# Eight stores of image rows issued in the next stage, and one square root moved between two copies

## The chip, the cores and the metric

The kernel runs on one core of a Trainium2 chip. The metric is the device time of one launch in microseconds (us), the median of several runs. A core has five engines, each with its own instruction stream: TensorE (PE in the rows; its weight loads are PEld), VectorE (DVE), ScalarE (ACT), GpSimd (POOL) and SyncE (SP), which in this kernel issues most of the DMAs. The engines wait for each other through semaphores only.

## The reference, cut to what matters

The model embeds 32 images and 32 texts and passes the joined rows through a mixer layer and a layer of 8 experts. The change lies in the embedding:

```python
x = x.reshape(B, C, h, P, w, P)                       # 32 images, 14 x 14 patches of 3 x 16 x 16
x = jnp.transpose(x, (0, 2, 4, 3, 5, 1)).reshape(B, h * w, P * P * C)
x = _layernorm(x, ln1_g, ln1_b)
x = jnp.einsum('bnp,pd->bnd', x, W_proj) + b_proj     # 768 -> 192
x = _layernorm(x, ln2_g, ln2_b)
x = jnp.concatenate([cls, x], axis=1) + pos_embedding
...
h = jnp.concatenate([image_rows, text_rows(x_txt, itok)], axis=1)
h = h + mixer(_layernorm(h))
h = h + experts(_layernorm(h))
```

## The kernel before, in words

The stages follow one another: embed_images, embed_text, normalise_in, mix, project_route, experts. Each is a function that opens one Block with an instruction list for each engine. At a Block's end all engines meet (a barrier, recorded on line 92 or 551 where the timeline names it), so a stage begins when the last engine has arrived.

embed_images takes the images in NGRP = 4 groups of GB = 8. Partition r of a tile holds patch row r // 8 of image r % 8, so a tile has 112 partitions. The 14 patch columns of a group are done one after the other, w = 0 to 13, in two alternating buffers. For each column

- ScalarE normalises the patches (normalise, L276);
- TensorE transposes them into PSUM (turn, L328, 6 transposes);
- ScalarE copies them out in two halves (take, L283 and L284); it waits for the transposes and for the projection two columns earlier;
- TensorE projects them (project, L336, 6 matmuls, recorded as 12 instructions); it waits for take of this column (turned_out) and for VectorE to have emptied the PSUM buffer of the column two before (y_taken);
- VectorE adds the bias into yg (y_take, L426) and gathers statistics (y_stat, L431).

The second normalisation needs the variance of the projected columns: VectorE computes it (y_moments, L403 to L410), ScalarE takes the square root (root_y, L289), VectorE the reciprocal (y_scales, L415) and then scales all columns (scale_mul L437, scale_add L444) and makes the statistics that the next stage wants (scale_stats, L451, which counts row_done). For the last group this is done in two parts, columns 0 to 9 (CUT = 10) and 10 to 13. VectorE's order at the end is: y_moments(0, CUT), take of columns 10 and 11, y_scales, then take of column 12 and the scaling of columns 0 to 9, take of column 13, and the second part.

SyncE writes yg to the intermediate h0 in DRAM: for each group eight DMAs, one an image (L220), for the last group eight for columns 0 to 9 when row_done says so, and eight for columns 10 to 13. yg and its completion semaphores y_out live on through embed_text. ScalarE at the end writes the class row (L318) and waits for that DMA.

In embed_text SyncE issues 12 small loads of weights (L631 to L643; among them win_row and wout_row, which TensorE transposes on L858 and L863), then waits for text rows to store (L649), and at its end waits for y_out. VectorE and TensorE build prefix sums, then text rows go in eight steps of four texts through ScalarE's Gelu (L818).

The order before at ScalarE's end of the image stage, and SyncE's:

```python
                if g + 1 == NGRP:
                    root_y(g, 0, CUT)
                for j in range(2):
                    take(g * GRID + GRID - 2 + j, j)
```

Of the kernel before, what the change touches and what calls it, by code (L numbers as in the profile page):

```python
# [29 lines left out]
GRID = IMG // PATCH  # L30
NIMG = GRID * GRID
# [3 lines left out]
LP = NCHUNK * Q  # L35
# [26 lines left out]
HR = D + 6  # L62
# [5 lines left out]
GB = 8  # L68
GP_ROWS = GB * GRID
NY = 3  # L70
NGRP = B // GB
PD = PATCH * PATCH * CH
BORDER = (0, 4, 1, 5, 2, 6, 3, 7)
# [4 lines left out]
def bank(nc, ctx, name, shape):  # L78

    t = ctx.enter_context(nc.psum_tensor(name, [128, 512], F32))  # L80
    n = 1
    for s in shape[1:]:
        n *= s
    v = t[0:shape[0], 0:n]
    if len(shape) == 3:
        v = v.rearrange("p (a b) -> p a b", a=shape[1])
    return v


def embed_images(nc, io, dr, keep):  # L90

    with ExitStack() as ctx:
# [3 lines left out]
        def sem(name):  # L96
            return ctx.enter_context(nc.semaphore(name))

        R = GP_ROWS
# [12 lines left out]
        yg = keep["yg"]  # L112
# [20 lines left out]
        vint = sb("vint", [128, 2, NVAR // 128], I32)  # L133

        ps_t = [[bank(nc, ctx, f"ps_t{j}{k}", [128, 3, R]) for k in range(2)]
                for j in range(2)]
        ps_y = [bank(nc, ctx, f"ps_y{j}", [R, D]) for j in range(2)]
        ps_b = bank(nc, ctx, "ps_b", [R, D])
        ps_i = bank(nc, ctx, "ps_i", [TXT, 2, B])

# [16 lines left out]
        row_done = sem("row_done")  # L157
        tick = keep["tick"]
        y_out = keep["y_out"]
# [19 lines left out]
        h0 = dr["h0"]  # L179
# [3 lines left out]
        @block.sync  # L183
        def _(sp):
            def whole(g):
                for b in BORDER:
                    sp.dma_start(xg[g][b:R:GB, :, :].rearrange("r (c p) w -> r c (p w)", c=CH),
                                 xv[g * GB + b].rearrange("h c p w -> h c (p w)")).then_inc(x_in[g % 2][0], 16)

            whole(0)  # L190
            sp.dma_start(vt[:, :, 0:NF], io["L0_txt_var_family_onehot"].rearrange("(p j) f -> p j f", p=128)
                          ).then_inc(tab, 16)
            for n, name in enumerate(["var_outer_norm", "var_inner_norm", "var_has_outer", "var_has_inner"]):
                sp.dma_start(vcol[:, n, :], io["L0_txt_" + name].rearrange("(p j) -> p j", p=128)).then_inc(tab, 16)
            for n, name in enumerate(["var_family_id", "var_group_id"]):
                sp.dma_start(vint[:, n, :], io["L0_txt_" + name].rearrange("(p j) -> p j", p=128)).then_inc(tab, 16)
            for b in BORDER:
                sp.dma_start(pos[b:R:GB, :, :].rearrange("r w d -> r (w d)"),
                             posv[0, 1:1 + NIMG, :].rearrange("(h w) d -> h (w d)", w=GRID)).then_inc(pos_in, 16)
            sp.dma_start(cls[:, 0, :], posv[0, 0, :].partition_broadcast(B)).then_inc(pos_in, 16)  # L200
            sp.dma_start(cls[:, 1, :], io["L0_tok_cls_token"][0, 0, :].partition_broadcast(B)).then_inc(pos_in, 16)
            whole(1)
            sp.wait_ge(tab, TAB_MADE)
            sp.dma_start(dr["var_tab"].rearrange("(p j) f -> p (j f)", p=128), vt[:].rearrange("p j f -> p (j f)")
                          ).then_inc(tab, 16)
            tables.store(sp)
            for g in range(2, NGRP):
                for n, (lo, hi) in enumerate(PIECES):
                    sp.wait_ge(x_normed, GRID * (g - 2) + hi)
                    for b in BORDER:  # L210
                        for c in range(CH):
                            sp.dma_start(xg[g % 2][b:R:GB, c * PATCH:(c + 1) * PATCH,
                                                   lo * PATCH:hi * PATCH],
                                         xv[g * GB + b][:, c, :, lo * PATCH:hi * PATCH]).then_inc(x_in[g % 2][n], 16)
            for g in range(NGRP):
                for lo, hi in ((0, GRID),) if g + 1 < NGRP else ((0, CUT), (CUT, GRID)):
                    sp.wait_ge(row_done, GRID * g + hi)
                    for b in BORDER:
                        row = (g * GB + b) * LP + 1
                        sp.dma_start(h0[row:row + NIMG, :].rearrange("(h w) d -> h (w d)", w=GRID)[:, lo * HR:hi * HR],  # L220
                                     yg[g % NY][b:R:GB, lo:hi, :].rearrange("r w d -> r (w d)")
                                     ).then_inc(y_out[min(g, 1)], 16)

        @block.gpsimd
        def _(pool):
# [29 lines left out]
        @block.scalar  # L255
        def _(act):
            for n, name in enumerate(("x_txt", "itok_BS_0_4095")):
                act.dma_start(idr[:, n, :], io[name]).then_inc(ids, 16)
            act.dma_start(wp[:, :, :, :].rearrange("p n c d -> p n (c d)"), wv).then_inc(w_in, 16)
            with nc.allow_non_contiguous_dma(reason="per-feature vectors of a few values"):  # L260
                act.dma_start(g1[:], gv).then_inc(w_in, 16)
                act.dma_start(b1[:], bv).then_inc(w_in, 16)
            for tile, name in ((bias1, "L0_tok_b_proj"), (g2, "L0_tok_ln2_g"), (b2, "L0_tok_ln2_b")):
                act.dma_start(tile[:], io[name].partition_broadcast(R)).then_inc(w_in, 16)
            act.wait_ge(misc, 1)
            act.dma_start(h0.rearrange("(b t) d -> b t d", t=LP)[:, L:LP, :].rearrange("b t d -> b (t d)"),
                          zrow[:]).then_inc(misc, 16)

            tables.functions(act)

            def root(g):
                act.wait_ge(x_std, g + 1)
                act.activation(rs[g % 2][:], ve[g % 2][:], ACT.Sqrt).then_inc(x_sqrt, 1)

            def normalise(g, w, j):
                act.activation(xc[j][:], xg[g % 2][:, :, bass.ds(w * PATCH, PATCH)], ACT.Identity,  # L276
                               bias=nb[g % 2][:, bass.ds(w, 1)], scale=rs[g % 2][:, bass.ds(w, 1)]
                               ).then_inc(x_normed, 1)

            def take(i, j):  # L280
                act.wait_ge(turned, i + 1)
                act.wait_ge(projected, i + 1)
                act.copy(xt[j][:, 0:3, :], ps_t[j][0][:])  # L283
                act.copy(xt[j][:, 3:6, :], ps_t[j][1][:]).then_inc(turned_out, 1)  # L284

            act.sem_inc(projected, 2)
            def root_y(n, lo=0, hi=GRID):
                act.wait_ge(y_var, n + 1)
                act.activation(rsy[:, lo:hi], vey[:, lo:hi], ACT.Sqrt).then_inc(y_sqrt, 1)  # L289

            def steps(g, lo, hi):
                with act.Fori(lo, hi) as p:
                    for j in range(2):
                        take(g * GRID + 2 * p + j, j)
                        normalise(g, 2 * p + 2 + j, j)

            root(0)
            act.wait_ge(x_rstd, 1)
            normalise(0, 0, 0)
            normalise(0, 1, 1)  # L300
            for g in range(NGRP):
                steps(g, 0, EARLY)
                if g:
                    root_y(g - 1)
                steps(g, EARLY, GRID // 2 - 1)
                if g + 1 == NGRP:
                    root_y(g, 0, CUT)
                for j in range(2):
                    take(g * GRID + GRID - 2 + j, j)
                    if g + 1 < NGRP:  # L310
                        if j == 0:
                            root(g + 1)
                            act.wait_ge(x_rstd, g + 2)
                        normalise(g + 1, j, j)
            root_y(NGRP, CUT, GRID)
            act.wait_ge(misc, 1 + 16)
            act.wait_ge(cls_ok, 1)
            act.dma_start(h0.rearrange("(b t) d -> b t d", t=LP)[:, 0, :], cls_row[:]).then_inc(misc, 16)  # L318
            act.wait_ge(misc, 1 + 32)
# [222 lines left out]
CUT = 2 * LATE  # L542
# [3 lines left out]
def embed_text(nc, io, dr, keep):  # L546
# [4 lines left out]
    with ExitStack() as ctx:  # L551
# [78 lines left out]
        def _(sp):  # L630
# [10 lines left out]
            sp.dma_start(wi[HD:HD + 1, 1, :], io["L0_attn_b_in"].unsqueeze(0)).then_inc(p_in, 16)  # L641
            for n in range(2):
                sp.dma_start(wout_row[:, n, :], io["L0_attn_W_out"][n * HD:(n + 1) * HD, :]).then_inc(p_in, 16)  # L643
            hv = dr["h0"].rearrange("(b t) d -> t b d", t=LP)
            for n in range(NG4):
                sp.wait_ge(rows_done, n + 1)
# [1698 lines left out]
```

## Time and profile before

| | us |
|---|---|
| median of 3 runs | 1410.48 (1410.46 to 1414.09) |
| the profiled execution's own time | 1408.07 |
| its span | 1406.3 |
| TensorE busy | 1166.0 (83%) |
| VectorE busy | 807.6 (57%) |
| ScalarE busy | 690.2 (49%) |
| GpSimd busy | 389.6 (28%) |

The profile comes from one execution. Times in it count from the span's start. A row of a timeline gives the start in us, the time in us from the beginning of the first to the end of the last of the instructions merged in it, engine, line, operation, the tile written and the tiles read, the number of instructions (x), and in brackets the engine's idle time before it with what ended it. SPq and ACTq are DMA issues on the queues of SyncE and ScalarE. The granted clock of TensorE is given as a share of full speed: 1.00 is 2.4 GHz, 0.50 is 1.2 GHz. Releasers are inferred from semaphore events.

### The profile page before, as it was taken

How to read it: one execution, taken by the hardware profiler on the slowest of the kernel's cores; microseconds unless marked ns; L12 is line 12 of the kernel's file. 1: busy time of each engine (PE TensorE's matmuls, PEld its weight loads, DVE VectorE, ACT ScalarE, POOL GpSimd, SP SyncE). 2: the span in 40 equal slices, each digit the busy share in tenths (PEclk: the TensorE clock that was granted, in tenths of full speed). 3: DMA queues.
4: the chain of work that ended last, by engine and by line, in shares of the span. 5: the costliest groups of instructions: out<-in, count | busy, mean ns of one | idle time of the engine just before them, and what ended most of it. 6: DMA issues, size and time to landing. Idle time of an engine off the chain costs nothing. (4 is left out here: it accounts for less than half of the span.)

```text
span 1406.3 us, 38278 instructions
## 1 busy us (share of the span) xinstructions
PE 1166.0 (83%) x11847; PEld 1098.3 (78%) x11847; DVE 807.6 (57%) x2553; ACT 690.2 (49%) x1544; POOL 389.6 (28%) x358
## 2 busy tenths in 40 slices
PE   0398993466579999999999499993799999999996
PEld 0398992244469898898898399983799999999996
DVE  0778976773842633534536368775455555666653
ACT  2265660255652332232233256652567777777774
POOL 6877000001100300201103015555123333333332
PEclk9999996576699998998999899995899999999998
DMA  8766312003410423333233689982111111111110
GB/s 189 178 102 147 98 36 68 23 0 121 209 27 14 92 79 76 69 99 77 64 98 80 185 255 305 296 256 79 33 43 42 45 42 42 45 45 45 45 45 13
DMA packets 166427, 133.83 MB, mean 95 GB/s; under 512 B 77989, under 2 KB 155932, under 8 KB 164704
## 3 DMA queue, kind: packets, MB, share of 16 engines
q1 hardware_dynamic: 152352, 112.22, 29.8%
q0 software_dynamic: 10384, 17.49, 3.9%
q10 hardware_dynamic: 3600, 3.01, 0.7%
q8 instruction: 45, 0.74, 0.2%
q14 instruction: 46, 0.38, 0.1%
HBM read 89.97 MB, written 43.53 MB: 95 GB/s over the span
## 5 line engine op out<-in xcount | busy, mean ns | idle before, releaser
L2125 POOL DMA_INDIRECT out_dram<-ob,oi x89 | 127.2, 1429 | 291.8 <-DVE ob L2179 288.8
L2235 PE MATMUL ph<-zt,wc 64*128 64x128 f32 x3204 | 197.4, 274 | 3.1 <-ACT zt L2137 1.4
L2235 PEld LDWEIGHTS ph<-zt,wc 64*128 64x128 f32 x3204 | 191.6, 189 | 6.9 <-issue 3.6
L2227 PE MATMUL py<-w2c,ht 64*128 64x192 f32 x2136 | 194.1, 327 | 1.5 <-DVE yb L2177 1.5
L1492 PE MATMUL pa<-wi,xn 96*85 (+3 forms) x2048 | 185.6, 246 | 3.0 <-POOL mc L1344 2.8
L1492 PEld LDWEIGHTS pa<-wi,xn 96*85 96x85 f32 (+1 forms) x2048 | 180.2, 155 | 4.4 <-POOL mc L1344 3.1
L2150 ACT ACTIVATE ht<-ph,bc 128x128 f32<-128x128 f32 x534 | 156.9, 371 | 48.5 <-PE ph L2235 48.5
L2227 PEld LDWEIGHTS py<-w2c,ht 64*128 64x128 f32 x2136 | 172.6, 187 | 2.0 <-issue 1.9
L1355 POOL TENSOR_TENSOR bd<-rr,mc 128x656 f32<-128x656 f32 x48 | 61.5, 1282 | 306.9 <-PE pb L1510 187.1
L1366 DVE COPY x<-pa 85x384 f32<-85x384 f32 x100 | 55.3, 553 | 146.0 <-PE pa L1492 146.0
L336 PE MATMUL ps_y<-wg,xt 128*112 128x192 f32 x672 | 124.2, 337 | 13.6 <-DVE yg L426 9.5
L2144 ACT COPY w2c<-w2e 128x1152 f32 x89 | 102.6, 1152 | 59.4 <-PE py L2227 59.0
L336 PEld LDWEIGHTS ps_y<-wg,xt 128*112 128x112 f32 x672 | 111.0, 183 | 15.2 <-DVE yg L426 10.5
L1538 PEld LDWEIGHTS pa<-gp,x 85*128 85x128 f32 x768 | 101.0, 207 | 15.0 <-issue 9.2
L1742 POOL DMA_INDIRECT xs<-row,sli x82 | 82.3, 1004 | 96.7 <-DVE row L1996 36.4
L1538 PE MATMUL pa<-gp,x 85*128 85x128 f32 x768 | 102.3, 292 | 7.4 <-issue 6.2
L1822 PE MATMUL p<-wo,y 128*128 128x192 f32 x492 | 93.0, 341 | 0.5 <-DVEq L1916 0.5
L1385 ACT ACTIVATE yt<-pa 96x384 f32<-96x384 f32 (+1 forms) x84 | 44.6, 531 | 98.8 <-PE pa L1552 91.3
L328 PE MATMUL ps_t<-ident,xc 112*128 112x112 f32 x336 | 43.2, 266 | 54.5 <-ACT xc L276 54.5
L1822 PEld LDWEIGHTS p<-wo,y 128*128 128x128 f32 x492 | 82.6, 197 | 0.7 <-DVEq L1916 0.7
L328 PEld LDWEIGHTS ps_t<-ident,xc 112*128 112x128 f32 x336 | 39.0, 146 | 56.1 <-ACT xc L276 54.7
L2164 DVE TENSOR_SCALAR z<-xr 128x192 f32<-128x192 f32 x89 | 33.8, 379 | 74.6 <-DMA xr<-xs 74.6
(318 smaller groups left out, 1966.2 us busy)
## 6 DMA issues: line engine op xcount, KB each, us to landing
y<-yd SPq DMA_DIRECT2D x41, 384.0 KB, 4.7
gp<-kd SPq DMA_DIRECT2D x48, 246.0 KB, 2.8
xg<-in_x SPq DMA_DIRECT2D x16, 588.0 KB
xr<-xs SPq DMA_DIRECT2D x89, 98.0 KB, 1.9
yd<-yt SPq DMA_DIRECT2D x56, 144.0 KB, 1.9
hb<-h SPq DMA_DIRECT2D x41, 192.0 KB, 5.6
yd<-yt SPq DMA_DIRECT2D x40, 192.0 KB, 2.1
xg<-in_x SPq DMA_DIRECT2D x48, 112.0 KB
```

What stands on the lines that cost most here:

```text
L328: t = pe.transpose(ps_t[j][k // 3][:, k % 3, :], flat[:, k * 128:(k + 1) * 128], keep["ident"][0:R, 0:R])
L336: m = pe.matmul(ps_y[j][:], xt[j][:, k, :], wg[:, k, :], start=(k == 0), stop=(k == KC - 1))
L1355: pool.tensor_tensor(bd[g % 2][:], rr[g % 2][:, :].unsqueeze(1).to_broadcast([128, GE, Q]), mc[:, bass.ds(n, 1), :].rearrange("p a e -> p ...
L1492: mm = pe.matmul(p[:, i * EB:(i + 1) * EB], xn[0:rows, f, b, c * Q:c * Q + W], keep["wi"][0:rows, f, bass.ds(k * EB, EB)], start=(f == 0), ...
L1538: mm = pe.matmul(p[:, i, :], x[:, g * GE + e, :], cols(g % 3, e), start=True, stop=True)
L1742: pool.indirect_dma_start(dr["xs"], bass.IndirectOffsetOnAxis(ap=sli[j][:, t:t + 1], axis=0), row[j][:, t, :], None, bounds_check=bound, o ...
L1822: m = pe.matmul(po[q % 2][:, i, 0:D], yt[q][:, k, 1 - i, :], keep["wo"][:, k, :], start=(k == 0), stop=(k == KO - 1))
L2125: pool.indirect_dma_start(out, bass.IndirectOffsetOnAxis(ap=oi[j][:, 0:1], axis=0), ob[j][:], None, bounds_check=bound, oob_is_err=False). ...
L2144: act.copy(w2c[j % 2][:], w2[:, :, bass.ds(ex * D, D)]).then_inc(act_ok, 1)
L2150: act.activation(ht[j][:, c, :], ph[c % 4][:, c // 4, :], ACT.Gelu, bias=bc[j][:, c:c + 1]).then_inc(act_ok, 1)
L2227: m = pe.matmul(py[h][:], ht[j][r, k, :], w2c[j % 2][r, k, :], start=(k == 0), stop=(k == FC - 1))
L2235: return pe.matmul(ph[c % 4][:, c // 4, :], wc[j][r, f:f + 128], zt[j][r, part, :], start=start, stop=stop, skip_group_check=True)
```

## The change

The stores of L220 become a helper, store_rows. SyncE's loop in the image stage issues columns 0 to 9 of the last group and ends; its eight DMAs for columns 10 to 13 are issued in embed_text, behind the 12 loads and before the first wait for text rows. They have no wait of their own there. And ScalarE's square root for columns 0 to 9 of the last group stands between its last two takes (of columns 12 and 13) instead of ahead of both.

```diff
+def store_rows(sp, h0, keep, g, lo, hi):
+    for b in BORDER:
+        row = (g * GB + b) * LP + 1
+        sp.dma_start(h0[row:row + NIMG, :].rearrange("(h w) d -> h (w d)", w=GRID)[:, lo * HR:hi * HR],
+                     keep["yg"][g % NY][b:GP_ROWS:GB, lo:hi, :].rearrange("r w d -> r (w d)")
+                     ).then_inc(keep["y_out"][min(g, 1)], 16)
...
             for g in range(NGRP):
-                for lo, hi in ((0, GRID),) if g + 1 < NGRP else ((0, CUT), (CUT, GRID)):
-                    sp.wait_ge(row_done, GRID * g + hi)
-                    for b in BORDER:
-                        row = (g * GB + b) * LP + 1
-                        sp.dma_start(h0[row:row + NIMG, :].rearrange("(h w) d -> h (w d)", w=GRID)[:, lo * HR:hi * HR],
-                                     yg[g % NY][b:R:GB, lo:hi, :].rearrange("r w d -> r (w d)")
-                                     ).then_inc(y_out[min(g, 1)], 16)
+                hi = GRID if g + 1 < NGRP else CUT
+                sp.wait_ge(row_done, GRID * g + hi)
+                store_rows(sp, h0, keep, g, 0, hi)
...
-                if g + 1 == NGRP:
-                    root_y(g, 0, CUT)
                 for j in range(2):
                     take(g * GRID + GRID - 2 + j, j)
+                    if g + 1 == NGRP and j == 0:
+                        root_y(g, 0, CUT)
...
             for n in range(2):
                 sp.dma_start(wout_row[:, n, :], io["L0_attn_W_out"][n * HD:(n + 1) * HD, :]).then_inc(p_in, 16)
+            store_rows(sp, dr["h0"], keep, NGRP - 1, CUT, GRID)
             hv = dr["h0"].rearrange("(b t) d -> t b d", t=LP)
```

## Rows read from the trace of the kernel before

**Rows 1.** Busy windows: from:to, length, busy PE, PEld, DVE, ACT, POOL, clock, DMA, GB/s.

```profile
226.00:234.20 8.20, 0.28 (x2) 0.00 (x0) 8.19 (x29) 0.00 (x0) 0.00 (x0) 0.84 0.00 1
...
247.80:347.80 100.00, 63.48 (x190) 39.59 (x190) 66.43 (x245) 43.94 (x83) 1.35 (x4) 0.67 0.12 40
347.80:1406.30 1058.50, 947.76 (x10635) 907.87 (x10635) 574.09 (x1803) 538.79 (x1276) 282.51 (x235) 0.94 0.33 95
```

**Rows 2.** Timeline of SyncE's DMA issues, last group of images.

```profile
234.20 6.41 SPq L220 DMA_DIRECT2D h<-yg  x8
...
240.66 6.41 SPq L220 DMA_DIRECT2D h<-yg  x8
```

**Rows 3.** Timeline of VectorE before and at the barrier.

```profile
231.50 2.68 DVE L451 BATCH_NORM_STATS2 yg<-yg 112x6 f32<-112x192 f32 x10
...
239.20 0.62 DVE L451 BATCH_NORM_STATS2 yg<-yg 112x6 f32<-112x192 f32 x2
247.85 0.21 DVE L676 COPY shi<-tk 128x32 f32<-128x32 f32 x1 [8.03 <-PEq L92]
```

**Rows 4.** DMA view, 234 to 242 us: tenths busy in 40 slices of 0.2.

```profile
DMA  0000000091139300910091009200920092009400
```

**Rows 5.** DMA view, issues: size, median us from issue to landing.

```profile
h<-cls_row ACTq DMA_DIRECT2D x1, 24.8 KB, 1.6
```

**Rows 6.** Timeline of PE, DVE and ACT from 212 to 236 us.

```profile
212.20 0.74 PE L328 MATMUL ps_t<-ident,xc 112*128 112x112 f32 x6
212.77 2.12 PE L336 MATMUL ps_y<-wg,xt 128*112 128x192 f32 x12
...
218.52 0.36 DVE L426 TENSOR_TENSOR yg<-ps_y,bias 112x192 f32<-112x192 f32 x1
218.62 0.21 ACT L289 ACTIVATE rsy<-vey 112x10 f32<-112x10 f32 x1 [6.47 <-DVE vey L410]
...
219.06 0.44 ACT L284 COPY xt<-ps_t 128x336 f32<-128x336 f32 x1
...
219.55 6.73 PE L336 MATMUL ps_y<-wg,xt 128*112 128x192 f32 x24 [4.09 <-ACT xt L284]
...
223.85 0.36 DVE L426 TENSOR_TENSOR yg<-ps_y,bias 112x192 f32<-112x192 f32 x1 [3.59 <-PE ps_y L336]
...
227.68 0.34 DVE L426 TENSOR_TENSOR yg<-ps_y,bias 112x192 f32<-112x192 f32 x1
...
235.18 0.33 ACTq L318 DMA_DIRECT2D h<-cls_row  x1
```

**Rows 7.** Windows of TensorE: length, busy, granted clock, DMA, GB/s.

```profile
218.00:220.00 2.00, 0.45 (x1) 0.50 0.51 133
...
224.00:226.00 2.00, 2.00 (x12) 0.80 0.40 105
...
230.00:232.00 2.00, 0.00 (x0) 0.91 0.00 0
```

**Rows 8.** Timeline of the text stage: loads, first use, first store.

```profile
252.38 0.78 SPq L643 DMA_DIRECT2D wout_row<-in_L_attn_W_out  x2
...
264.60 0.20 PEld L858 LDWEIGHTS ph<-ident,win_row 128*96 128x96 f32 x1
...
323.25 0.40 SPq L649 DMA_DIRECT2D h<-ott  x1
```

**Rows 9.** DMA view, 252 to 258 us: tenths busy in 40 slices of 0.15.

```profile
DMA  1112865489999985455410004000000000000000
```

**Rows 10.** Line L818, Gelu: duration ns min/median/max, starts of first and last.

```profile
L818 ACT ACTIVATE htt<-ph,bbt x2: 682/682/682, 301.3 to 305.2; 64x512 f32<-64x512 f32 x2
...
L818 ACT ACTIVATE htt<-ph,bbt x2: 682/682/682, 332.5 to 337.2; 64x512 f32<-64x512 f32 x2
```

**Rows 11.** Windows of TensorE in the text stage, columns as in group 7.

```profile
301.30:305.10 3.80, 3.13 (x15) 1.00 0.00 0
324.00:341.50 17.50, 17.50 (x44) 0.50 0.41 140
```

## The prediction

> **What bounds the kernel now.** I read four things in this order. The busy windows by stage [rows 1] say where the time is: an image stage to 247.8 us, a text stage of 100 us, and 1058.5 us behind it in which TensorE is busy 90% of the time (947.76 of 1058.50). The change touches the end of the first stage and the beginning of the second. A barrier lies between the stages and another behind the text stage, so what is saved before a barrier moves everything behind it, one for one, unless another engine now arrives late. Then the timeline at the barrier [rows 2, 3]: VectorE's last instructions end at 239.20 + 0.62 = 239.82, and it does nothing until 247.85. What fills these 8.03 us is SyncE alone: eight stores issued from 234.20 for 6.41 us (0.80 each), eight more from 240.66 for 6.41, to 247.07, and some 0.75 us later the text stage starts. The chain of 16 issues is unbroken and begins when VectorE has finished columns 0 to 9 of the last group (their statistics end at 231.50 + 2.68 = 234.18). So the stage's end is VectorE's column chain up to 234.18, and from there SyncE's issuing. It is not the data: the DMA digits in steps of 0.2 us [rows 4] show a short burst every 0.8 us and engines at rest between bursts. Last, ScalarE, TensorE and VectorE from 212 to 236 and the granted clock there [rows 6, 7], for the second edit.
>
> **Part one, the stores of columns 10 to 13.** Eight DMAs leave the image stage and are issued in the text stage behind its 12 loads; their wait on row_done goes, since the barrier stands for it. Without them SyncE is done at 234.20 + 6.41 = 240.61, and the text stage starts 0.74 us later, at 241.35 and not at 247.81: 6.46 us less. Who could then be later than SyncE? VectorE ends at 239.82, 0.79 before it. ScalarE issues the class row's DMA at 235.18 [rows 6] and waits for it; it lands 1.6 us after its issue [rows 5], near 237. TensorE's last matmul ends at 219.55 + 6.73 = 226.28 [rows 6]. SyncE stays the last, so the part is worth 6.46 if the barrier costs the same. Bounds: 5.7 with a barrier twice as dear, 7.2 with one that is free.
>
> What it adds in the text stage: 8 issues x 0.80 = 6.4 us of SyncE behind the loads, which are out at 252.38 + 0.78 = 253.16 [rows 8], so up to 259.6 in the old kernel's times. Nothing queued behind them on SyncE is due before its first text store at 323.25, 64 us later [rows 8], and the final wait on these stores stands at the end of the stage, some 88 us later. The loads stay ahead of the stores in SyncE's order. The last ones, win_row and wout_row, occupy the DMA engines until about 255.7 [rows 9]; TensorE first reads win_row at 264.60 [rows 8]. That is 9 us of cover, against eight bursts that each fill the engines for some 0.2 to 0.4 us [rows 4], 3.2 us at most. I cost the addition at nothing; if the cover were gone, each us of lateness would cost one.
>
> **Part two, ScalarE's root** [rows 6]. Before its last two takes (each is the two copies of one column's transposed patches) ScalarE waits 6.47 us for VectorE's variances, from 212.15 to 218.62. The root runs, the take of column 12 ends at 219.06 + 0.44 = 219.50, and TensorE starts the projection of column 12 at 219.55, released by that copy. In the new order this take needs only TensorE's transposes, done at 212.20 + 0.74 = 212.94. It is over near 213.8, almost 5 us before the root's input exists, so the root is not delayed. What ends last for the projection is then its other wait, VectorE's removal of column 10 from the same PSUM buffer: 218.52 + 0.36 = 218.88, and with the 0.05 us from release to matmul that the old order shows (219.50 to 219.55) it starts at 218.93: **0.62 us** earlier. VectorE sat idle 3.59 us for this projection (to 223.85) and then is busy 8.19 of 8.20 us up to 234.20 [rows 1], so this moves the rest of its chain and SyncE's first issue with it. The take of column 13 follows the root, as before it followed the take of column 12, and ends near 219.6, over 3 us before its projection.
>
> Bounds of part two. The projection took 4.30 us (219.55 to 223.85) at a granted clock of 0.50, which is 1.2 GHz, and one took 2.12 at 1.00, 2.4 GHz (at 212.77) [rows 6, 7]. If the clock had not fallen, 2.18 more would be gained: 2.8 in all. If instead the last projection ran at the low clock too (218.93 + 2 x 4.30 = 227.53), VectorE, which would want it at 227.68 - 0.62 = 227.06, would wait 0.47. So from 0.15 to 2.8. I take 0.62: TensorE's gap before it reaches from 215.46 (219.55 - 4.09) to 218.93 and still covers 218, where the clock had fallen, and it rose again only at about 224.8 (0.80 between 224 and 226).
>
> The low clock is not tied to one idle length: it fell here within 2.6 us of the last transpose, and a few us later stayed up through about 5.3 us of idleness (226.28 to 231.6, from 0.91 between 230 and 232) [rows 7]. I take the pattern of clock changes as free to move in the new kernel, and two rivals below price that. The Trainium skill (TensorE: Matmul & The Clock Gate, Part 1: The HAM clock gate) says that the gate runs freely and doesn't start with the kernel, so that the point of change varies from run to run. By that rule the fall at 218 need not come again; then the sum would be 9.3 and not 7.1, and the trace, one execution, can't say how often.
>
> **Sum.** 6.46 + 0.62 = 7.08 us. The profiled execution took 1408.07 us (span 1406.3); changed, it would take 1401.0. The median of the three timed runs is 1410.48, 2.4 above it, and they reach from 1410.46 to 1414.09. The metric is the median, so I subtract there: 1410.48 - 7.08 = **1403.4**.
>
> **Rivals.**
> *A, the clock gives more.* The projection keeps the high clock (2.2 more), or the text stage does better. There one step from Gelu to Gelu takes 3.9 us at 1.00 (301.3 to 305.2) and 4.7 at 0.50 (332.5 to 337.2), and from 324 to 341.5 TensorE was busy throughout at 0.50 [rows 10, 11]. Four such steps at the high clock save 3.2. With either or both, 1398.0 to 1401.2, say 1400. For it: both levels occur in the stage and a shift of 7 us may deal them anew. Against: the same holds for the other side.
> *B, the clock takes back.* Four steps that ran at 1.00 fall to 0.50: 4 x 0.8 = 3.2, with the 0.47 of part two 3.7, so 1407.1. The same evidence, mirrored.
> *C, the change doesn't bring the barrier forward,* because SyncE's issues don't hold it. Then only part two's 0.62 is left, 1409.9. It needs another arrival near 247; the rows show none, and the start so close behind SyncE's last issue speaks against it.
> *D, slower: the stores delay the text stage's weights.* Place: TensorE's transposes of win_row and wout_row at 264.60, with ScalarE's copies and the stage's projections behind them. Price: one for one from the point at which the loads land over 9 us later than now. At 9 + 7.1 = 16 us the change is slower than before, at 20 us measurably (1415). Against it: engines at rest between bursts, and the loads ahead of the stores in SyncE's order.
>
> **How the numbers follow.** The forecast, within about 2 us: 0.70. The same with part two worth nothing (1404.0): 0.04. A: 0.10. B: 0.10. C: 0.04. D: 0.02. A measurement of this kernel can tell about 0.3%, 4.2 us, from no change, so below 1406.2 is faster. Faster: 0.74, A's 0.10, and 0.03 of B, where fewer than four steps fall: 0.87. Same: the rest of B, and C: 0.11. Slower: D, 0.02. The range goes from 1398.5, most of A, to 1408.0, B's 1407.1 and a little for the spread of the runs; C, D and the tail of A are left out.
>
> **What would show it.** Right: the text stage starts some 0.75 us after SyncE's eighth store of columns 0 to 9, near 240.7; VectorE's idleness at the barrier falls from 8.03 us to about 1.6; ScalarE's copies for column 12 stand near 213, its root still near 218.6, and the projection of column 12 starts near 218.9, released by VectorE. Eight store issues stand behind the load of wout_row, over by 252.5; TensorE reads win_row about 17 us into the stage, as before; the stage is 100 us long, give or take 4. Wrong: a text stage longer by several us at an unchanged clock pattern, a barrier well behind SyncE's last issue, or a projection released later than VectorE's removal of column 10.

## The result and the profile after

The changed kernel takes 1403.14 us (median of 12 runs, 1400.38 to 1408.01), the kernel before 1410.82 (12 runs, 1402.74 to 1414.09). The ratio is 0.9954, with a 95% interval of 0.9935 to 0.9973: 6.5 us less, between 3.8 and 9.2. The forecast was 1403.4. The ratio takes in all executions and differs a little from that of the two medians. Each kernel below was timed beside the kernel before, whose median there is given with it.

The profiled execution took 1405.35 us, with a span of 1403.6. The timeline of SyncE's DMA issues around the barrier, which answers to [rows 2] (the helper store_rows records its issues on line 94):

```profile
232.58 6.41 SPq L94 DMA_DIRECT2D h<-yg  x8
...
239.73 0.32 SPq L636 DMA_DIRECT2D w1t<-in_L_txt_W  x1
...
244.30 0.78 SPq L648 DMA_DIRECT2D wout_row<-in_L_attn_W_out  x2
245.12 6.99 SPq L94 DMA_DIRECT2D h<-yg  x8
...
314.32 21.45 SPq L655 DMA_DIRECT2D h<-ott  x8
...
339.04 2.06 SPq L1096 DMA_DIRECT2D h<-h  x4
```

The eight stores of columns 0 to 9 end at 232.58 + 6.41 = 238.99, the text stage's first issue comes 0.74 us later, and the eight others follow the loads there and end 62 us before the next thing on that queue is due. The timeline of VectorE, ScalarE and TensorE, which answers to [rows 3, 6]:

```profile
212.37 0.44 ACT L288 COPY xt<-ps_t 128x336 f32<-128x336 f32 x1 [0.83 <-PE ps_t L333]
...
217.91 0.36 DVE L431 TENSOR_TENSOR yg<-ps_y,bias 112x192 f32<-112x192 f32 x1
218.01 0.21 ACT L294 ACTIVATE rsy<-vey 112x10 f32<-112x10 f32 x1 [4.87 <-DVE vey L415]
...
218.41 5.81 PE L341 MATMUL ps_y<-wg,xt 128*112 128x192 f32 x24 [3.55 <-DVE yg L431]
...
222.23 0.36 DVE L431 TENSOR_TENSOR yg<-ps_y,bias 112x192 f32<-112x192 f32 x1 [2.58 <-PE ps_y L341]
...
237.58 0.62 DVE L456 BATCH_NORM_STATS2 yg<-yg 112x6 f32<-112x192 f32 x2
...
239.77 0.21 DVE L682 COPY shi<-tk 128x32 f32<-128x32 f32 x1 [1.57 <-PEq L101]
```

ScalarE takes column 12 at 212.37, before the root and not behind it; TensorE's projection at 218.41 is released by VectorE and no longer by ScalarE's copy; VectorE's idleness at the barrier is 1.57 us where [rows 3] had 8.03.

Spans of single executions don't compare well here. To see where the time went in each trace, the following table takes one landmark (an instruction that every kernel has) for each stage: the root of the first ten columns, VectorE's first instruction of the text stage (the start of text), the first load of normalise_in, GpSimd's first memset in mix, its first iota in project_route, and the table load at which ScalarE enters the experts. The numbers are lengths between landmarks in us, all from the timelines.

| kernel | root at | root to text | text | normalise | mixer | project, route | experts to end |
|---|---|---|---|---|---|---|---|
| before | 218.62 | 29.23 | 100.00 | 56.5 | 394.1 | 188.7 | 419.2 |
| after | 218.01 | 21.76 | 99.27 | 56.4 | 396.9 | 190.6 | 420.7 |
| after, again (r_after) | 217.88 | 21.39 | 99.64 | 56.4 | 396.7 | 189.3 | 418.1 |
| after, third (r2_after) | 218.62 | 22.21 | 99.70 | 56.6 | 397.1 | 190.0 | 421.8 |
| e1 stores only | 218.21 | 22.22 | 99.20 | 56.4 | 394.7 | 190.8 | 420.4 |
| e2 root only | 217.66 | 28.37 | 98.91 | 56.4 | 396.9 | 188.7 | 417.9 |
| e3 all in text | 217.50 | 19.00 | 99.78 | 56.1 | 396.6 | 189.8 | 419.3 |
| e5 sixteen ahead | 217.95 | 18.98 | 100.60 | 56.3 | 395.7 | 189.6 | 421.1 |
| e8 twenty-four ahead | 218.47 | 20.48 | 107.05 | 56.4 | 395.6 | 190.7 | 424.0 |
| e6 busy | 218.68 | 20.23 | 100.44 | 56.4 | 402.5 | 189.5 | 421.4 |
| e7 all and busy | 219.79 | 18.97 | 99.57 | 56.1 | 401.3 | 192.3 | 422.8 |
| e9 padding, nine | 219.08 | 21.83 | 98.80 | 56.5 | 400.9 | 190.2 | 421.6 |
| e11 padding, fifteen | 218.27 | 22.21 | 97.23 | 56.4 | 397.1 | 190.5 | 422.4 |
| e10 busy, padded | 218.41 | 18.99 | 97.35 | 56.3 | 396.7 | 190.9 | 419.4 |

From root to text the change takes away 29.23 - 21.76 = 7.47 us. The text stage then starts 8.08 us earlier, 0.61 of which was there before the root and has nothing to do with the change. At the end only 2.7 us of it are left. The stages behind lost them (mixer 2.8, project and route 1.9, experts 1.5), and e2, which keeps all 16 stores in the image stage, has the long mixer too. From the mixer on the three traces of the changed kernel add up to 1008.1, 1004.1 and 1008.8 us, a scatter of 4.7 for one kernel, against 1001.9 and 1003.6 in the traces of before and e2; e1, e3, e5 and e8 lie at 1005.7 to 1010.2.

So all seven traces with the stores moved and no extra matmuls stand above the two without the move, which looks like a loss behind the text stage. But the traced executions are not typical of their kernels: those of before and e2 took 2.8 and 1.4 us less than their kernel's median, those of after, r_after and r2_after 2.2, 0.5 and 5.5 us more. If these differences arose behind the text stage, then without them it is 1004.7 and 1005.0 us for before and e2 and 1005.9, 1003.6 and 1003.3 for the changed kernel (an estimate), and no loss is left. The times leave little room for one too: by the ratios of its three timings (0.9954 here, 0.9931 and 0.9949 below) the changed kernel is 6.5, 9.7 and 7.2 us faster, 7.8 on average, where the trace has 7.47 up to the text stage.

### The profile page after: what moved, and what is told of

It is laid out like the page before. It is cut to its first block and busy times, and to the rows that moved or that the text cites. A ratio compares the mean times of both kernels' runs of the same rounds, so it can differ in the third digit from the quotient of the medians.

```text
span 1403.6 us, 38278 instructions
## 1 busy us (share of the span) xinstructions
PE 1165.1 (83%) x11847; PEld 1098.4 (78%) x11847; DVE 807.2 (58%) x2553; ACT 689.7 (49%) x1544; POOL 390.5 (28%) x358
## 5 line engine op out<-in xcount | busy, mean ns | idle before, releaser
L1391 ACT ACTIVATE yt<-pa 96x384 f32<-96x384 f32 (+1 forms) x84 | 44.5, 530 | 98.9 <-PE pa L1558 91.4
```

## The experiments

**The two halves, and the change again.** e1 keeps the root in its old place:

```diff
+                if g + 1 == NGRP:
+                    root_y(g, 0, CUT)
                 for j in range(2):
                     take(g * GRID + GRID - 2 + j, j)
-                    if g + 1 == NGRP and j == 0:
-                        root_y(g, 0, CUT)
```

> The change's first half alone: the eight stores of columns 10 to 13 in the text stage, ScalarE's root in its old place. Theory (the barrier waits for SyncE's issues): the text stage starts about 0.75 us after SyncE's eighth store of columns 0 to 9, VectorE's idleness at the barrier is about 1.6 us and not 8.0, and the whole is 6.5 us below the kernel before. Rival (something else holds the barrier near its old time, and the gain came from elsewhere): the idleness at the barrier stays near 8 us and the time within 1 us of the kernel before.

Measured: 1403.58 us against 1408.70 (0.9951, 0.9932 to 0.9971). SyncE and VectorE at the barrier:

```profile
233.24 6.41 SPq L94 DMA_DIRECT2D h<-yg  x8
240.38 0.32 SPq L636 DMA_DIRECT2D w1t<-in_L_txt_W  x1
...
240.43 0.21 DVE L682 COPY shi<-tk 128x32 f32<-128x32 f32 x1 [1.57 <-PEq L101]
```

From root to text it is 29.23 - 22.22 = 7.01 us shorter. The projection of column 12 took 3.74 us here (219.14 to 222.88) and 4.30 in [rows 6], by the clock; without these 0.56 us 6.45 are left for the stores, and 6.46 were worked out. The rival (the idleness at the barrier stays near 8 us) is out.

e2 is the kernel before with the root's move alone (between the takes); the stores stay as they were.

> The change's second half alone: the root between the last two takes, all 16 stores in the image stage. Theory: the projection of column 12 starts about 0.05 us after VectorE's removal of column 10 ends (0.6 us earlier relative to it than in the kernel before), SyncE's first store follows 0.6 us earlier relative to the root, the barrier idleness stays near 8 us, and the whole gains 0.6 us, too little to be told in the times. Rival (the move shifts TensorE's clock and brings the 1 us more that the changed kernel's trace shows): the projection takes under 4 us again in this kernel, and 1 us or more is gained at the barrier.

Measured: 1408.18 us against 1408.70 (0.9991, 0.9979 to 1.0002), not to be told from no change. In the trace the 16 stores stand as one block and the idleness is the old 8.03 us:

```profile
232.38 12.87 SPq L220 DMA_DIRECT2D h<-yg  x16
245.99 0.32 SPq L631 DMA_DIRECT2D w1t<-in_L_txt_W  x1
```

Root to text is 0.86 us shorter. The projection starts 0.39 us behind the root's start (218.05 and 217.66) instead of 0.93 [rows 6]: 0.54. The remaining 0.32 are the projection itself, 3.98 us and not 4.30. Of the rival's two signs one is just met (a projection under 4 us) and the other is not (1 us or more gained). e1, with the root in its old place, has a still shorter projection (3.74 us): this term belongs to the clock and not to the move.

r_after is the changed kernel unaltered.

> The changed kernel once more, beside the three others. If the 8.8 us that its first trace was ahead at the end of the text stage, and the 6 us of it that were gone at the end, are chance of single executions (clock pattern, landings of transfers in the stages behind), this trace is again 7 to 9 us ahead at the end of the text stage, and at the end by another amount than 2.7 us; the times stay 7 us below the kernel before. If the loss behind the text stage belongs to the change, the later stages are again 6 us longer than in the first trace of the kernel before.

Measured: 1400.79 us against 1408.70 (0.9931, 0.9907 to 0.9955). At the end of the text stage this trace is 8.94 us ahead of the first trace of before (338.91 and 347.85), and at the end of the span 6.9. It is the expected case for chance.

**What holds the barrier after the change.** e3 stores all columns of the last group in the text stage, with eight DMAs behind the loads (and the stage's last wait is for 16 * GB * (NGRP - 1)):

```diff
-            for g in range(NGRP):
-                hi = GRID if g + 1 < NGRP else CUT
-                sp.wait_ge(row_done, GRID * g + hi)
-                store_rows(sp, h0, keep, g, 0, hi)
+            for g in range(NGRP - 1):
+                sp.wait_ge(row_done, GRID * (g + 1))
+                store_rows(sp, h0, keep, g, 0, GRID)
...
-            store_rows(sp, dr["h0"], keep, NGRP - 1, CUT, GRID)
+            store_rows(sp, dr["h0"], keep, NGRP - 1, 0, GRID)
```

> The changed kernel, but all 14 columns of the last group are stored in the text stage, by eight DMAs behind the loads; none of the 16 issues is left in the image stage. Theory (after the change SyncE is still the last to arrive, VectorE 0.79 us ahead of it): the barrier is now held by VectorE, the text stage starts 0.75 us after its last instruction, 0.8 us earlier than in the changed kernel relative to that engine's chain, and the whole gains 0.8 us over the changed kernel. Rival (the barrier costs more once VectorE is last, or ScalarE's class row holds it): the text stage starts 1.5 us or more after VectorE's last instruction and nothing is gained.

Measured: 1399.03 us against 1408.70 (0.9938, 0.9916 to 0.9961), the same as r_after beside it within the intervals; the 0.8 us expected are too few for the times to show. The trace shows VectorE as the last:

```profile
235.55 0.62 DVE L455 BATCH_NORM_STATS2 yg<-yg 112x6 f32<-112x192 f32 x2
236.50 0.21 DVE L681 COPY shi<-tk 128x32 f32<-128x32 f32 x1 [0.33 <-PEq L101]
```

VectorE's first instruction of the text stage comes 0.33 us after its last one. Behind SyncE's last store it came 0.78 us later (238.99 to 239.77; SyncE's own next issue 0.74). So these 0.78 us are not the barrier's price whoever comes last: 0.45 of them go when VectorE is the last, and the distance left by the change is 1.57 - 0.33 = 1.24 us and not 0.79. Root to text is 19.00, 2.76 less than in the trace of after; 1.24 of that is the barrier, and 1.53 is the projection (2.29 us from its start to VectorE's next removal, 3.82 in the trace of after), for here the clock did not fall. These windows of TensorE give length, busy time, granted clock and DMA, first for after, then for e3:

```profile
218.00:220.00 2.00, 1.59 (x7) 0.72 0.60 155
220.00:222.00 2.00, 2.00 (x8) 0.50 0.89 233
```

```profile
216.00:218.00 2.00, 0.10 (x1) 1.00 0.17 39
218.00:220.00 2.00, 2.00 (x13) 1.00 0.72 194
```

The gap is as long as in after (3.55 us). So whether the clock falls there is chance: of the nine traces with this gap of 3.55 us left empty, it fell in seven, in some within the gap and in others only in the first us of the projection, and stayed up in two (e3 and e5). The first clock rival is seen in single executions, up to 2 us of it. In the text stage, where both rivals put 3 us, the six traces of before, after, e1, e2, e3 and r_after lie between 98.9 and 100.0 us.

**How much delay the weights can bear.** The prediction gave the loads 9 us of cover and said that every further us would cost one. e5 issues all 16 stores of the last group in front of the loads:

```diff
+            store_rows(sp, dr["h0"], keep, NGRP - 1, 0, CUT)
+            store_rows(sp, dr["h0"], keep, NGRP - 1, CUT, GRID)
             sp.dma_start(w1[:], io[T + "W1"]).then_inc(w_in, 16)
...
-            store_rows(sp, dr["h0"], keep, NGRP - 1, CUT, GRID)
```

> All 16 stores of the last group are issued in the text stage, and ahead of its 12 loads, so that the loads go out 16 x 0.80 = 12.8 us later in the stage. TensorE reads win_row 16.8 us into the stage and the loads are there 7.9 us into it, 8.9 us of cover. The prediction's price (one for one beyond 9 us): the text stage is 4 us longer. Rival (the cover is larger than TensorE's wait shows, since ScalarE idles another 3.5 us behind its copies of these weights before its next input is there, and VectorE doesn't wait for them): TensorE reads win_row near 21 us into the stage, and the stage is at most 0.5 us longer.

e8 puts the eight stores of the third group in front of these too.

> As the kernel with 16 stores ahead of the loads, with the eight stores of the third group ahead of them too: the loads go out 24 x 0.80 = 19.2 us later in the stage. The prediction's price: the stage is 19.2 - 8.9 = 10.3 us longer. Rival, with ScalarE's 3.5 us: 19.2 - 8.9 - 3.5 = 6.8 us longer.

Measured, both against 1409.91: e5 1403.16 us (0.9956, 0.9935 to 0.9978), its text stage 100.60 long; e8 1411.54 us (1.0023, 0.9996 to 1.0049), its text stage 107.05. Against the 99.27 to 99.70 of the three traces of after that is 0.9 to 1.3 and 7.4 to 7.8 us longer. The first line here is TensorE's first read of win_row in e5 (text starts at 236.93), the second ScalarE's root behind the weights, with no idleness before it; the third and fourth are the same in e8 (text starts at 238.95):

```profile
258.54 1.08 PEld L864 LDWEIGHTS ph<-ident,win_row 128*96 128x96 f32 x6 [4.97 <-DMA wout_row<-in_L_attn_W_out]
...
261.68 0.21 ACT L800 ACTIVATE vet<-vet 128x8 f32<-128x8 f32 x1
```

```profile
266.97 1.09 PEld L865 LDWEIGHTS ph<-ident,win_row 128*96 128x96 f32 x6 [11.39 <-DMA wout_row<-in_L_attn_W_out]
...
270.12 0.21 ACT L801 ACTIVATE vet<-vet 128x8 f32<-128x8 f32 x1
```

In e5 TensorE waits and reads win_row 21.6 us into the stage instead of 16.8, 4.8 us late. ScalarE's root of the text stage comes at 24.75 and not at 23.55 (271.40 - 247.85), only 1.2 us late: in the kernel before, ScalarE had idled 3.49 us for this root's input, as its line there shows:

```profile
271.40 0.21 ACT L794 ACTIVATE vet<-vet 128x8 f32<-128x8 f32 x1 [3.49 <-DVE vet L737]
```

So the cover is the 9 us in front of TensorE's read and ScalarE's 3.5 us behind it, some 12 us. The rival's 0.5 and 6.8 us are near the 0.9 to 1.3 and 7.4 to 7.8 measured, the 4 and 10.3 of one-for-one are not. What was missing is in the issues: 16 and 24 stores held the first load back by 13.6 us (236.93 to 250.50) and 19.9 us (238.95 to 258.84) where 12.8 and 19.2 were worked out, and with these the rival's sum gives 1.2 and 7.5. Behind the cover each us does cost one: in e8 all that the change brings is gone. That it becomes slower than the kernel before isn't shown, since e8's interval reaches from 0.9996 to 1.0049.

**TensorE's gap.** e6 fills it with nine matmuls of constant tiles, whose result nobody reads:

```diff
             turn(n - 1, 1)
+            for k in range(9):
+                pe.matmul(ps_b[:], b1w[:, k % KC, :], wg[:, k % KC, :], start=(k == 0), stop=(k == 8))
             project(n - 2, 0)
```

> The changed kernel with nine extra matmuls of two constant tiles in TensorE's gap ahead of the last two projections (into a PSUM bank that nothing reads any more; about 3.2 us at the high clock, the gap is 3.55). Theory (the projection of column 12 takes 3.3 to 4.3 us instead of 2.1 only because the clock had fallen in that gap, and VectorE waits for it): the clock stays at 1.00, the projection takes 2.1 to 2.3 us, VectorE waits 1.1 us or less, and the text stage starts 1.0 to 1.7 us earlier behind the root. Rival (the extra matmuls delay the projection or the clock falls all the same): nothing gained or up to 1 us lost.

e7 is the same edit on e3.

> All stores of the last group in the text stage behind the loads, and the extra matmuls in TensorE's gap: candidate for the fastest. Theory: the text stage starts 0.3 us after VectorE's last instruction and about 19 us after the root, as in the run with all stores in the text stage, where the clock had risen early by chance; about 3 us below the changed kernel. Rival (only one of the two gains is had): 1.3 us below it.

Measured, both against 1409.91: e6 1409.15 us (0.9998, 0.9977 to 1.0019), e7 1405.72 us (0.9983, 0.9962 to 1.0005). In the gap both do what was expected. TensorE, then VectorE in e6:

```profile
215.37 3.09 PE L363 MATMUL ps_b<-wg,b1w 128*112 128x192 f32 x18
...
219.07 4.12 PE L341 MATMUL ps_y<-wg,xt 128*112 128x192 f32 x24 [0.61 <-DVE yg L433]
...
221.36 0.36 DVE L433 TENSOR_TENSOR yg<-ps_y,bias 112x192 f32<-112x192 f32 x1 [1.05 <-PE ps_y L341]
```

The projection takes 2.29 us, root to text is 20.23 (21.39 to 22.21 in the traces of after) and 18.97 in e7. But the whole doesn't gain, it loses: by the ratios e6 stands 6 to 9 us above the changed kernel and e7 some 6 us above e3. By the table most of it is in the mixer: 402.5 and 401.3 us, where the nine traces without extra matmuls have 394.1 to 397.1. The timeline of TensorE there has it, at the two places where its loop over the channel blocks starts again ("issue": the engine waited for nothing that the profile shows). First r_after, then e6:

```profile
536.52 7.18 PE L1544 MATMUL pa<-gp,x 85*128 85x128 f32 x32 [2.67 <-issue]
...
634.93 6.65 PE L1544 MATMUL pa<-gp,x 85*128 85x128 f32 x32 [2.35 <-issue]
```

```profile
537.19 0.79 PE L1546 MATMUL pa<-gp,x 85*128 85x128 f32 x2 [3.06 <-issue]
539.99 6.77 PE L1546 MATMUL pa<-gp,x 85*128 85x128 f32 x30 [2.00 <-issue]
...
638.72 0.62 PE L1546 MATMUL pa<-gp,x 85*128 85x128 f32 x2 [2.78 <-issue]
641.64 6.77 PE L1546 MATMUL pa<-gp,x 85*128 85x128 f32 x30 [2.30 <-issue]
```

At each restart TensorE stops once in the changed kernel and twice in e6, the second time two recorded matmuls further on. The extra matmuls stand 300 us earlier; what they change there is only the place of all later instructions in TensorE's stream. Three kernels test that. e9 is the changed kernel with the nine matmuls behind the last projection, where TensorE waits for the barrier anyway:

```diff
             project(n - 1, 1)
+            for k in range(9):
+                pe.matmul(ps_b[:], b1w[:, k % KC, :], wg[:, k % KC, :], start=(k == 0), stop=(k == 8))
```

> The changed kernel with the same nine extra matmuls, but behind TensorE's last projection, where it waits for the barrier in any case. They touch no stage in time; what they change is that every later TensorE instruction stands nine matmuls further back in its stream. Theory (the mixer stage is 6 us longer with the extra matmuls because TensorE, at each of the two restarts of its loop there, stops twice for instructions and not once): the mixer stage is 402 us long and not 396.7, with a second stop of about 2 us two matmuls behind each restart, and the whole is 6 us above the changed kernel. Rival (the extra matmuls in the gap shifted the clock or the transfers): the mixer stage is 396 to 397 us and the whole equals the changed kernel.

e11 has 15 of them there.

> As the run with nine extra matmuls behind the last projection, with 15 of them. Theory (the second stop stands at a fixed place of the stream, which with nine falls two matmuls behind the loop's head; 24 more instructions push the loop's head past it): one stop at each restart, the mixer stage back to 396 to 397 us, the whole equal to the changed kernel. Rival (more instructions cost more, wherever they stand): the mixer stage as long as with nine, or longer.

e10 is e7 with six more behind the last projection, 15 in all.

> Candidate for the fastest: all stores of the last group in the text stage, nine extra matmuls in TensorE's gap so that the clock stays up, and six more behind the last projection. Theory: the text stage starts 19.0 us behind the root (21.4 to 21.8 in the changed kernel), the mixer stage has one stop at each restart and is 396 to 397 us long; about 2.5 us below the changed kernel. Rival (the mixer stage stays at 401 us): 2 to 3 us above it.

> The changed kernel once more on the same chip as the three others, as their common measure: about 7 us below the kernel before, text stage 21.4 to 22 us behind the root, mixer stage 396 to 397 us.

Measured, on one chip, where the kernel before takes 1410.06: r2_after 1402.21 us (0.9949, 0.9923 to 0.9975), e9 1409.59 us (0.9986, 0.9972 to 1.0000), e11 1406.23 us (0.9965, 0.9949 to 0.9981), e10 1400.35 us (0.9926, 0.9906 to 0.9945). TensorE at the restarts in e9, then in e11:

```profile
539.90 6.77 PE L1546 MATMUL pa<-gp,x 85*128 85x128 f32 x30 [1.85 <-issue]
...
641.53 6.77 PE L1546 MATMUL pa<-gp,x 85*128 85x128 f32 x30 [2.46 <-issue]
```

```profile
535.26 7.16 PE L1546 MATMUL pa<-gp,x 85*128 85x128 f32 x32 [2.64 <-issue]
...
634.12 7.05 PE L1546 MATMUL pa<-gp,x 85*128 85x128 f32 x32 [2.81 <-issue]
```

Nine matmuls that cost nothing where they stand make the mixer 400.9 us long, with the second stop; fifteen give 397.1, with one. It is the place in the stream and not the number of instructions, nor the clock in the gap.

The traces also show what the stops go with. The profile lists a DMA queue that carries instructions, in 45 packets of 16 KB:

```profile
q8 instruction: 45, 0.74, 0.2%
```

At each of the 28 first stops of the 14 traces such a packet starts 0.1 to 0.6 us before the stop, and TensorE goes on 1.9 to 2.0 us after it has landed. At each of the six second stops (e6, e7, e9) the next packet starts 0.1 to 0.3 us after TensorE went on, and TensorE goes on again 1.2 to 1.5 us after that one has landed; in e9 it runs from 537.51 to 538.51, and the stop from 538.05 to 539.90. In the other traces a next packet starts 0.1 to 0.8 us after the stop as well, and TensorE doesn't wait for it. The profile doesn't say which engine the packets are for, but this pattern is that of a wait for instructions.

For e11's whole the expectation missed: its mixer is as it should be, and its median is still 4 us above that of r2_after, with overlapping ranges (1400.6 to 1410.6 and 1395.8 to 1408.8). Its experts stage (422.4) is at the upper end of the table. Whether another loop lies badly there, or it is scatter, stays open.

e10 has both gains: 18.99 from root to text, one stop at each restart. Its median is 1.9 us below that of r2_after, its interval overlaps. The traces show 2.4 to 3.2 us taken out ahead of the text stage; the times alone can't rank e10, e3 and the changed kernel.

## Why the prediction was right

**The bound.** It rested on the barrier being held by SyncE's issues. e1 alone gives 6.45 us where 6.46 were worked out. The rows that decided it were [rows 2 to 4], the unbroken chain of issues 0.8 us apart and engines at rest between bursts.

**Who is late next.** SyncE, as forecast, with VectorE's idleness at 1.57 us where about 1.6 was named. But to set VectorE's end against SyncE's (0.79 us ahead) takes the barrier to cost the same whoever comes last, and it doesn't: to VectorE's next instruction it is 0.78 us behind SyncE and 0.33 behind VectorE (e3). So VectorE had not 0.79 us to spare but 1.24, and the whole of the last group's stores moved would have been worth 6.45 + 1.24 = 7.7 us. For the change itself this didn't matter, since SyncE stayed the last.

**What it adds.** Nothing, as costed. The eight issues took 6.99 us in the text stage of after, and 6.5 to 7.6 in other traces, instead of 6.41, without anyone waiting. The price behind the cover was mis-sized: the cover is some 12 us and not 9 (e5, e8), since the prediction asked only who waits for the weights and not whether that one is waited for in turn.

**The root.** 0.54 us in e2 instead of 0.62. The term that was off is the step from release to matmul: with VectorE's removal ending at 217.91 + 0.36 = 218.27 the projection starts at 218.41, 0.14 us later, where 0.05 was taken from a release by ScalarE. Root in place and released by VectorE, as forecast.

**The clock.** The projection took 4.30 us in the trace of before, 3.82 in after, and 2.29 in e3 and e5, which have after's gap. The bound of 2.18 us for it held (4.30 - 2.29 = 2.01), and it is chance, as assumed. That the pattern in the text stage might move by 3 us either way is borne out in part. In the ten traces that have the loads first and at most nine extra matmuls the stage stayed within 1.7 us (98.80 to 100.44), at a mean granted clock of 0.67. In the two kernels with 15 extra matmuls it is shorter (97.2 and 97.4), at 0.69: the full clock holds from about 289 to 313 us in e11 and 286 to 310 in e10, where the others drop to half once on the way (after from 300.8 to 304.2 us). So rival A's second part exists, at some 2 us of its 3.2, in other kernels than the changed one; whether the extra matmuls bring it, or chance, was not tried.

**The sum.** Root to text: 6.45 for the stores, 0.54 for the root and 4.30 - 3.82 = 0.48 of clock make the 7.47 measured; 7.08 was forecast. The step from there to the median held as well (7.7 us between the medians, 6.5 by the ratio), though a single pair of executions showed 2.7. That the median came within 0.3 us of the forecast is luck: the interval of the measured ratio is 2.7 us to either side, the three timings of the changed kernel put the gain at 6.5, 9.7 and 7.2 us, and in the traced sum an unforecast 0.48 of clock stands beside terms that came out 0.09 low. The mechanism is shown apart from that, by the barrier in e1, e2 and e3.

## What to carry to other kernels

Where all engines leave a stage together, look at who arrives last and what it was doing: issuing DMAs is work of the issuing engine, here 0.8 us each, and can go behind the barrier if the data stay alive and the queue there has time. To price a delay of a transfer, follow it past its first reader until someone is met who would really be late. And compare a small edit by stage lengths and not by whole spans: an edit that adds or removes instructions can lengthen a loop far behind it, which the same edit with another amount of padding shows.

## What the runs showed of the hardware that was not expected

- The restart of a long TensorE loop costs a stop of 2.3 to 3.1 us in which it waits for nothing that the profile shows; where the loop's head stands in the instruction stream decides whether there is a second one of 1.8 to 2.5 us, two recorded matmuls on. Nine matmuls of padding 300 us earlier brought it in, fifteen took it out (mixer 396.7 to 397.1, 400.9, 397.1 us). Each of the 28 first stops ended 1.9 to 2.0 us after a 16 KB packet of instructions had landed, each of the six second ones 1.2 to 1.5 us after.
- VectorE's first instruction behind the barrier comes 0.78 us after the end of SyncE's last DMA issue when SyncE is the last to arrive (after), and 0.33 us after VectorE's own last instruction when VectorE is (e3).
- The same 3.55 us of TensorE idleness went with a fall to the half clock in seven traces and with the full clock in two, 1.2 to 2 us of difference for the engine that waits (3.45 to 4.26 against 2.29 us for the projection).
